# Attention scores in fewer rows, two heads side by side in row tiles of 64

## The reference

```python
xs = xn.reshape(B, C, H * W).transpose(0, 2, 1)          # 784 tokens of 64 channels, 32 images
qkv = (xs @ w_proj.T + b_proj).reshape(B, H * W, N_HEADS, 3 * D_K)   # 4 heads, D_K = 16
q, k, v = jnp.split(qkv, 3, axis=-1)
attn = jnp.einsum('bihk,bjhk->bijh', q, k) * D_K ** 0.5
attn = jax.nn.softmax(attn, axis=2)
h = jnp.einsum('bjhk,bijh->bihk', v, attn)
h = h.reshape(B, H * W, N_HEADS * D_K) @ w_out.T + b_out
h = h * jax.nn.sigmoid(h) + xs
```

## Time and profile before

| what | value |
|---|---|
| median of 3 executions | 1867.15 us (1853.65 to 1873.03) |
| the profiled execution | 1864.64 us, span 1862.8 us |
| mean granted clock of TensorE | 0.946 |
| TensorE busy | 1698.2 us, 91% |
| VectorE busy | 1284.5 us, 69% |
| ScalarE busy | 1022.3 us, 55% |
| GpSimd busy | 433.9 us, 23% |

### The profile page before, as it was taken

The page is one execution under the profiler, slowest core; times in us unless marked ns, Lnnn a source line. Parts: engine busy times, 40 slices in busy tenths (PEclk is TensorE's granted clock), DMA queues, the critical chain, the costliest instruction groups (busy, mean ns, idle before and its releaser), DMA issues.

```text
span 1862.8 us, 35089 instructions
## 1 busy us (share of the span) xinstructions
PE 1698.2 (91%) x10910; PEld 743.9 (40%) x10910; DVE 1284.5 (69%) x2603; ACT 1022.3 (55%) x1401; POOL 433.9 (23%) x333
## 2 busy tenths in 40 slices
PE   0799959999686799999999999999999999999997
PEld 0222225545585244444434443443443443344432
DVE  5466537788687687777767667776776777767762
ACT  0000126676232157777767666666776776766776
POOL 1300011111300303324224232241332423324111
PEclk9999979999898689999999999998999999999998
DMA  8111136666000424223322342222322232224300
GB/s 193 30 40 40 49 57 98 110 102 109 2 0 1 61 37 57 32 42 51 53 42 33 50 61 35 42 37 45 53 45 42 40 60 47 32 41 54 50 11 19
DMA packets 70267, 93.31 MB, mean 50 GB/s; under 512 B 22648, under 2 KB 63224, under 8 KB 69968
## 3 DMA queue, kind: packets, MB, share of 16 engines
q1 hardware_dynamic: 67728, 89.59, 29.4%
q0 software_dynamic: 2368, 1.57, 1.0%
HBM read 9.00 MB, written 6.42 MB: 8 GB/s over the span
## 4 chain that ended last, share of the span: by engine, by line
PE 81%; DVE 6%; ACT 4%; DMA 3%; SPq 3%; issue 3%; DVEq 0%; POOL 0%; ACTq 0%; POOLq 0%
PE ps L1051 19%; PE ps L1041 17%; PE ps L986 16%; PE ps L861 9%; PE ps L885 5%; PE ps L900 3%; PE ps L1032 3%; PE ps L1007 2%; ACT arena L679 2%; DMA x<-x_in 2%; PE ps L947 2%; SPq L433 1%; PE ps L1024 1%; DVE arena L1430 1%; PE ps L1015 1%
## 5 line engine op out<-in xcount | busy, mean ns | idle before, releaser
L1430 DVE TENSOR_REDUCE arena<-ps 128x1 f32<-128x392 f32 x1600 | 827.2, 560 | 329.6 <-PE ps L986 316.6
L792 ACT ACTIVATE arena<-ps 112x784 f32<-112x784 f32 x896 | 703.5, 822 | 270.5 <-PE ps L1041 265.8
L986 PE MATMUL ps<-arena 112*128 112x392 bf16 x1536 | 490.8, 348 | 8.7 <-DMA arena<-arena 8.3
L1041 PE MATMUL ps<-arena 114*112 114x392 bf16 x1792 | 457.2, 342 | 20.1 <-issue 15.1
L1051 PE MATMUL ps<-arena 112*32 112x392 f32 x3584 | 402.3, 521 | 0.0
L986 PEld LDWEIGHTS ps<-arena 112*128 112x128 bf16 x1536 | 151.2, 99 | 378.0 <-DVE arena L1430 307.9
L1041 PEld LDWEIGHTS ps<-arena 114*112 114x112 bf16 x1792 | 230.3, 136 | 140.8 <-issue 51.1
L861 PE MATMUL ps<-arena 128*64 128x392 f32 (+1 forms) x768 | 169.8, 553 | 3.9 <-DMA arena<-arena 3.9
L885 PE MATMUL ps<-arena 96*128 96x392 f16 x768 | 144.3, 339 | 22.1 <-DMA arena<-arena 16.7
L679 ACT ACTIVATE arena<-ps,magic,arena 128x784 f32<-128x784 f32 x128 | 128.2, 1005 | 39.4 <-PE ps L885 39.2
L1051 PEld LDWEIGHTS ps<-arena 112*32 112x32 f32 x3584 | 71.5, 109 | 147.6 <-issue 146.0
(11 more groups left out here) (139 smaller groups left out, 1394.8 us busy)
## 6 DMA issues: line engine op xcount, KB each, us to landing
arena<-arena SPq DMA_DIRECT2D x504, 73.5 KB, 2.7
arena<-arena SPq DMA_DIRECT2D x256, 84.2 KB, 2.8
x<-x_in SPq DMA_DIRECT2D x8, 784.0 KB, 21.2
out<-x SPq DMA_DIRECT2D x16, 392.0 KB, 2.4
arena<-arena SPq DMA_DIRECT2D x252, 24.5 KB, 2.4
arena<-arena SPq DMA_DIRECT2D x256, 1.5 KB
arena<-arena SPq DMA_DIRECT2D x16, 225.0 KB, 3.4
arena<-arena SPq DMA_DIRECT2D x16, 224.8 KB, 2.9
```

The source lines that it names most:

```text
L792: nc.scalar.activation(probs[w % 2][:, 2 * pair:2 * pair + 2, :], two(2 * place, rows=slice(0, TT)), ACT.Exp).then_inc(s_taken, 1)
L986: last = nc.tensor.matmul(ps[:, bank, 0:CH], q[0:ROWS_L, h, it * 128:(it + 1) * 128], k[0:ROWS_L, h, c * CH:(c + 1) * CH], start=True, sto ...
L1041: last = nc.tensor.matmul(ps[0:TT, 2 * place + j, 0:CH], ks[s % 4][0:ROWS_ALL, h, jt * TT:(jt + 1) * TT], qs[s % 4][0:ROWS_ALL, h, c * CH: ...
L1430: nc.vector.tensor_reduce(mx[img % 2][:, c, v:v + 1], scores, AX.X, ALU.max).then_inc(s_mf, 1)
```

## The change

q and k are scaled to a common top (from a bound computed out of the weights at the start), and split into two float16 parts, high and low. A product over 48 rows (high by high, high by low, low by high; 3 times 16) replaces that over 112, and two rows with minus the maximum make 50. Heads 0 and 1 lie in partitions 0 to 49, heads 2 and 3 in partitions 64 to 113, so that two products use the two halves of the array's rows and write two banks. The scores of a unit are one such pair. A unit of maxima becomes an event: one half of the keys for 128 queries of two heads, again a pair, which fills two of the three banks; both products stand together ahead of the weighing product, and `halfway` is gone. The last 16 queries of all heads are copied into a block tile of their own (`q_tail`, two transfers per image) and need four products of 64 columns.

The maxima are now joined and split into parts ahead of the transpose (VectorE), ScalarE copies the transposed parts as float16, and 6 transfers send them where 10 did; `stack` has 8 transfers for 24. GpSimd splits with two operations per tensor for four, and its order of `spread`, split and `gather` changes. The exponential gets its scale from a tensor. "den" stands behind unit 14 in even and 15 in odd steps, the reciprocals behind unit 9 in both.

```diff
-ROWS_HM, ROWS_L, ROWS_ALL = DK * 6, DK * 7, DK * 7 + 2
+ROWS_HH, ROWS_S, ROWS_ALL = DK * 2, DK * 3, DK * 3 + 2
+QK_TOP, GN_TOP, MAX_UNIT = 2048.0, 40.0, 4096.0
...
-        U_RECIP = 9, 18
-        U_DEN = 14, 24
+        U_RECIP = 9, 9
+        U_DEN = 14, 15
...
-        MROW_DMAS = 2 * (NH + 1)
-        STACK_DMAS = 6 * NH
+        MROW_DMAS = 2 * 2 + 2
+        STACK_DMAS = 2 * 4
+        TAIL_DMAS = 2
...
+                for half in range(2):
+                    r = im * C + half * 2 * DK
+                    q, k = qk_parts[r:r + DK], qk_parts[r + DK:r + 2 * DK]
+                    at = half * C
+                    sp.dma_start(qs[to][at:at + ROWS_HH, :, :].rearrange("p h t -> p (h t)"),
+                                 q[:, 0:1].rearrange("p k h t -> p k (h t)").to_broadcast([DK, 2, 2 * T])
+                                 ).then_inc(s_stack[im], 16)
+                    sp.dma_start(qs[to][at + ROWS_HH:at + ROWS_S, :, :], q[:, 1]).then_inc(s_stack[im], 16)
+                    sp.dma_start(ks[to][at:at + ROWS_HH, :, :].rearrange("p h t -> p (h t)"),
+                                 k.rearrange("p k h t -> p k (h t)")).then_inc(s_stack[im], 16)
+                    sp.dma_start(ks[to][at + ROWS_HH:at + ROWS_S, :, :], k[:, 0]).then_inc(s_stack[im], 16)
...
                         nc.scalar.activation(probs[w % 2][:, 2 * pair:2 * pair + 2, :],
-                                             two(2 * place, rows=slice(0, TT)), ACT.Exp).then_inc(s_taken, 1)
+                                             two(2 * place, rows=slice(0, TT)), ACT.Exp,
+                                             scale=score_scale[0:TT, 0:1]).then_inc(s_taken, 1)
...
-            def max_chunk(img, v, j, m, c, after_short=False):
-                k = 2 * j + c
-                if k >= MAX_BANKS:
-                    pe.wait_ge(s_mf, 2 * m + (c + 1 - MAX_BANKS))
-                elif k < 2 and not (isinstance(m, int) and m == 0):
-                    pe.wait_ge(s_mf, 2 * m + (0 if after_short else c - 1))
...
+            def max_event(img, e, j, m, tails=TAIL_DMAS * 16):
+                if j > 0:
+                    pe.wait_ge(s_mf, 2 * m - 1)
+                elif not (isinstance(m, int) and m == 0):
+                    pe.wait_ge(s_mf, 2 * m)
+                banks = [BANK_MAX + (2 * j + k) % MAX_BANKS for k in range(2)]
...
+                    for half in range(2):
+                        rows = slice(half * C, half * C + ROWS_S)
+                        last = nc.tensor.matmul(ps[:, banks[half], 0:CH], q[rows, h, it * 128:(it + 1) * 128],
+                                                k[rows, h, c * CH:(c + 1) * CH], start=True, stop=True)
...
-                for j in range(2):
-                    h = 2 * pair + j
+                for half in range(2):
+                    rows = slice(half * C, half * C + ROWS_ALL)
                     last = nc.tensor.matmul(
-                        ps[0:TT, 2 * place + j, 0:CH], ks[s % 4][0:ROWS_ALL, h, jt * TT:(jt + 1) * TT],
-                        qs[s % 4][0:ROWS_ALL, h, c * CH:(c + 1) * CH], start=True, stop=True)
+                        ps[0:TT, 2 * place + half, 0:CH], ks[s % 4][rows, pair, jt * TT:(jt + 1) * TT],
+                        qs[s % 4][rows, pair, c * CH:(c + 1) * CH], start=True, stop=True)
...
+                link(v.tensor_tensor(mx_all[:, :], mx[img % 2][:, 0, :], mx[img % 2][:, 1, :], ALU.max))
+                link(v.tensor_scalar(mx_high[:, :], mx_all[:, :], -1.0 / MAX_UNIT, None, ALU.mult))
+                high = mx_high.rearrange("p (g t) -> p g t", t=QT)
+                v.tensor_copy(mx_parts[:, :, 0, :], high)
+                v.scalar_tensor_tensor(mx_parts[:, :, 1, :], mx_all.rearrange("p (g t) -> p g t", t=QT),
+                                       -1.0 / MAX_UNIT, high, ALU.mult, ALU.subtract).then_inc(s_mx, 1)
```

More of the change, by code:

```diff
@@ L33 @@
 DEN_ROWS = 28
+VG = NH + 2
+V_TAIL = NH * QT
 EPS = 1e-5
@@ L154, in build @@
         xs = part([128, T])
[L155 to L163, removed]
+        qk32 = part([128, 2, T])
+        qk_parts = part([128, 2, 2, T], F16)
+        mx = [part([128, 2, VG * QT]) for _ in range(2)]
+        mx_all = part([128, VG * QT])
+        mx_high = part([128, VG * QT], F16)
+        mx_parts = part([128, VG, 2, QT])
+        negm = part([VG * 2 * QT, 128], F16)
         heads = [part([128, T]) for _ in range(4)]
@@ L242, in build @@
         s_stack = [sem(f"s_stack{n}") for n in range(2)]
-        s_first_k = sem("s_first_k")
+        s_top = sem("s_top")
+        s_topv = sem("s_topv")
+        s_tail = [sem(f"s_tail{n}") for n in range(2)]
         s_mrow = sem("s_mrow")
@@ L436, in _, with stack @@
             pair_steps(shift_step, sp)
[L439 removed]
+            def stack(im, s, i):
                 to = (s + 3) % 4
[L442 to L451, removed]
[L452 to L454 removed]
@@ L603, in l3_pool @@
                 num = lin(lambda t: t, s, i, 4)
-                between = [lambda: spread(s - 1, lin(lambda t: 2 * t, s, i, 4)), lambda: gather(num)]
-                if s == 0:
-                    between = [lambda: None] * 2
                 if has_qk(s):
@@ L817, in _ @@
             pe.wait_ge(s_par, 16)
+            pe.wait_ge(s_topv, 1)
+            for k in range(2):
+                last = nc.tensor.matmul(ps[:, 2, k:k + 1], abs_w[:, k * 128:(k + 1) * 128], top_in[:, 0:1],
+                                        start=True, stop=True)
+            last.then_inc(s_top, 1)
+            pe.wait_ge(s_topv, 2)
+            nc.tensor.matmul(ps[0:1, 2, 128:256], top_abs[:, 3:4], P("ident"), start=True, stop=True).then_inc(s_top, 1)
+            pe.wait_ge(s_topv, 3)
+            nc.tensor.matmul(ps[:, 2, 256:258], P("one_row", 1), top[0:1, :], start=True, stop=True).then_inc(s_top, 1)
             group_stats(0)
@@ L1003, in qk_product @@
[L1003 to L1006, removed]
-                    last = nc.tensor.matmul(ps[:, 2 * place + c, 0:CH], P(name), xs[:, c * CH:(c + 1) * CH],
-                                            start=True, stop=True)
+                    last = nc.tensor.matmul(ps[:, 2 * place + c, 0:CH], P("wqk")[:, k * 128:(k + 1) * 128],
+                                            xs[:, c * CH:(c + 1) * CH], start=True, stop=True)
```

286 lines of the change are left out of this document (150 added, 136 removed).

## The result

The changed kernel takes 2015.97 us (median of four runs, 2011.78 to 2030.42), the kernel before, in the same comparison, 1860.4 us (1848.8 to 1873.03). The ratio is 1.0849, with a 95% interval of 1.0749 to 1.0948: slower by 8.5%. The profiled execution took 2030.42 us, its span is 2028.6.

A forecast was written before the change was run, and what follows sets the result against it. The prediction took TensorE to bound the kernel, in the attention stage (1185 of 1862.8 us). It summed 1864.6 - 32 (rest of the images) + 0 (start) + 87 (clock) = 1920 us, range 1815 to 1990.

The forecast's parts named there:

- the clock's term: Attention stage: clock falls behind nearly every denominator product and slows the pairs that follow; +87 us, taken between 0 and +185.
- The term of the rest: Attention stage, clock aside: eleven ordinary pairs, open pairs, projections and denominators together -1.0 us per image, -32 us over 32.
- My upper end: Attention stage: 188 pairs at the low clock, 1.19 us more each, +224 us, less 39 for earlier falls: +185.
- The ordinary pair: Attention stage, two steps with maxima: 2.22 to 2.32 us where they cost 2.25; 3.41 us at the low clock.
- The join: VectorE, before the transpose of the maxima: three operations of some 0.2 us are added, costed at nothing in the loop.
- The start: Start of the attention stage: fewer splits and transfers against slower first maxima; together 0, within 5 us.
- The scale from a tensor: ScalarE's exponentials: reading the scale from a tensor adds 0.09 us each, mostly beside TensorE's work.
- The clock returning at once: Rival, pairs behind the denominator product: clock recovers at once, same layout without the 87 us; 1833 us, chance 0.26.
- no overlap: Rival, TensorE's row tiles: two tiles run one behind the other, 2.7 us per ordinary pair; 2000 us, chance 0.09.
- VectorE's pace: Rival, ordinary pairs: four VectorE reductions set the length, 1.9 to 1.95 us; 1727 us in all, chance 0.09.

## Why the prediction was wrong

**The direction and the mechanism held, the size of the clock's term didn't.** The step that failed is this one: "I take a bit under the middle, +87, since the q product and steps without maxima may lift it earlier". The stage has 619 us of low time, each worth 1 - 2.27/3.46 = 0.344: 213 us, less the 39 that the time before held, +174. That is 87 us more than I took. The term of the rest was too good by some 22 (below), and 1920 + 87 + 22 = 2029 is the profiled execution (2030.42). My upper end was +185, and 1864.6 - 32 + 185 would have been 2018, beside the measured median of 2015.97. That closeness is partly luck: +185 is 11 too high, -32 some 22 too low, and the median lies 14 below the profiled execution from which +174 is read. Every denominator product takes the clock down, and in even images it stays down to the output product, as the upper end assumed; the run with that product moved shows that it ends the fall. In odd images the doubt had a ground: steps without maxima lift the clock early in 8 of 16. But 3 of these fall again, and the even images and the other odd ones are at full length, so little is saved. The q product comes in no low stretch.

The rows already spoke for the upper end. From 628 to 662 us one 112-row product per reduction had held the clock at 0.50 for 34 us; the pair after the change, with thinner tiles and a wait per pair, is nearer to that stretch than to the one that rose, and I took the middle between them for want of a row in between.

**The ordinary pair**: predicted 2.22 to 2.32, measured 2.27; at the low clock 3.41 and 3.46. The loop from reduction to maxima product was laid out rightly, and the halves apart gave 0.2 us a pair back. Row tiles overlap, as taken. In the first image's maxima, events were to follow each other every 1.16 us; they do every 1.17:

```profile
640.35 0.11 PEld L1011 LDWEIGHTS ps<-arena 48*128 48x128 f16 x2 [1.07 <-DVE arena L1469]
...
641.52 0.11 PEld L1011 LDWEIGHTS ps<-arena 48*128 48x128 f16 x2 [1.07 <-DVE arena L1469]
```

**The rest of an image**: -32 us taken. The pairs at the high clock show it without the clock. Over two images their medians add up to 71.3 us in the run with the 128-row product alone, the join's gap with them, for 71.9 in the kernel before: -0.3 per image, some -10 us, not -32. The open pairs with nothing else in them gain more than was taken (1.43 to 1.52 us for 1.90), but longer projections and denominators take it back: 4.14 us for 3.56 with q or k, 4.08 for 3.56 with the odd image's denominator at the high clock.

**The join** stood in the prediction as "three operations of some 0.2 join before the transpose", at nothing. There are four, and they stand between two reductions on which TensorE's next maxima wait. In even images, with 0.2 us each, they start no fall, as taken. What was missed is that in odd images GpSimd's product runs beside the first, which then takes up to 0.99 us. In the changed kernel this is mostly hidden behind the other cause; without that it costs 91 us, nearly all through the clock. "I expect none there", of falls in ordinary pairs, was right for the pairs and wrong for this gap in them.

**The start** (0, within 5) came out at -2: from the stage's first q product to the first scores it is 57.3 us (610.05 to 667.30) for 59.0 (603.83 to 662.80). That the q product itself begins 6 us later is no effect of the change: with the same instructions ahead of it, it begins at 608.80 in the run with the spread join and at 602.59 in that with the 128-row product alone. **The scale from a tensor** (0.09 per exponential, beside TensorE) was right: 91 ns, nothing in the time.

**The rivals.** The clock returning at once is out (0.77 in the stage, not 0.95), and so is no overlap. VectorE's pace is real only with the halves apart: the pair is then 2.07, not 1.9 to 1.95, as a reduction in a row costs 0.52 and not 0.47. By this alone 1727 was some 40 us too low (2.07 for 1.95 in eleven pairs of 32 images).

## What to carry over

Where a trace shows the clock falling behind a thin product, price a change by how long each fall will last: find the next block of products over all rows behind it, and count the steps between at the low clock, at full length, unless a row shows that the products between lift it. Fill the thin product's rows with zeros first; that was 2.2 to 2.5% of this kernel, part of it without the clock, and took one memset. And before thinning an engine's products, lay out the loop of waits around them: a pair of products that shares one wait on another engine, and small operations that stand between that engine's reductions, decide what the thinner work is worth. For such small operations look at what runs beside them: five times their length came from an operation on GpSimd.

## What the hardware showed unexpectedly

- A maximum of two 128 x 36 tensors on VectorE takes 0.19 to 0.20 us alone and up to 0.99 us where it starts during GpSimd's 128 x 784 product (1.83 to 1.87 us). In the changed kernel this happens 15 times, at different points of that product: the maximum takes 0.37 to 0.99 us and each time ends 0.05 to 0.06 us behind it. So it waits for the product's end. In the run with the join moved away from it, the mean over all 32 is 0.19. No run varied it alone.
- Between row tiles the float32 denominator product takes 1.58 us over 4 rows and 1.59 over 128, four passes each at the high clock, but the clock holds behind the full one. Between products over 112 rows the pair with the 4-row one is 0.62 us longer, clock aside.
- TensorE shown busy 39.63 of 40 us can have a mean clock of 0.64.
